# Two quotient buffers in a quantised feed-forward, its tile loop reordered, and its weights turned earlier

## The reference

```
x = x + attention_0(layernorm(x), ctx)      # 16 heads of 16, softmax, biases
x = x + experts(layernorm(x))               # 32 experts + 8 zero experts, 6 per token
x = x + attention_1(layernorm(x), ctx)
x = x + fp4_ffn(layernorm(x))

def fp4_quant_dequant(x):                   # blocks of 16 along the last dimension
    scale = maximum(max(abs(xb)) / 6, 1e-12)
    idx = searchsorted([.25,.75,1.25,1.75,2.5,3.5,5], abs(xb / scale))
    return [0,.5,1,1.5,2,3,4,6][idx] * sign(xb) * scale

gate, up = fp4_linear(x, w_gate), fp4_linear(x, w_up)     # 256 -> 704
fp4_linear(silu(gate) * up, w_down)                       # 704 -> 256
```

## Time and profile before

| what | value |
|---|---|
| median of 3 runs | 998.67 us (998.26 to 1001.34) |
| the profiled execution | 1005.61 us, its span 1003.8 us |
| mean granted TensorE clock | 0.951 |
| TensorE busy | 898.1 us, 89% |
| VectorE busy | 626.4 us, 62% |
| ScalarE busy | 437.4 us, 44% |
| GpSimd busy | 304.1 us, 30% |
| feed-forward, from the weights' turns to the last sum | 837.8 to 1001.4 us |

### The profile page before, as it was taken

The page is one execution under the profiler, slowest core; times in us unless marked ns, Lnnn a source line. Parts: engine busy times, 40 slices in busy tenths (PEclk is TensorE's granted clock), DMA queues, the critical chain, the costliest instruction groups (busy, mean ns, idle before and its releaser), DMA issues.

```text
span 1003.8 us, 19829 instructions
## 1 busy us (share of the span) xinstructions
PE 898.1 (89%) x7228; PEld 685.1 (68%) x7228; DVE 626.4 (62%) x1317; ACT 437.4 (44%) x946; POOL 304.1 (30%) x311
## 2 busy tenths in 40 slices
PE   2997799999997978999999967799999996699996
PEld 1764687878876747878888844587878874366664
DVE  3455577878854594545545465566777764678872
ACT  0442466666664561111111112466666675345442
POOL 8003466767782260000000004000000001476673
PEclk9998799999998798999999977999999999999998
DMA  9788644444333469121111204345565500000000
GB/s 258 219 238 203 113 93 92 93 93 93 62 106 98 138 214 250 46 67 32 32 32 48 65 3 82 74 85 112 107 117 109 106 27 21 0 11 16 16 10 22
DMA packets 98157, 90.45 MB, mean 90 GB/s; under 512 B 43554, under 2 KB 85410, under 8 KB 97954
## 3 DMA queue, kind: packets, MB, share of 16 engines
q1 hardware_dynamic: 98066, 89.25, 36.6%
HBM read 69.36 MB, written 19.63 MB: 89 GB/s over the span
## 4 chain that ended last, share of the span: by engine, by line
PE 72%; DVE 12%; DMA 5%; POOL 3%; ACT 3%; issue 2%; SPq 2%; DVEq 0%; POOLq 0%; ACTq 0%
PE ps L988 13%; PE ps L805 8%; PE ps L859 8%; PE ps L791 8%; PE ps L994 7%; PE ps L819 7%; PE ps L1062 3%; DMA Qz<-mT 3%; PE ps L709 3%; PE ps L1078 2%; PE ps L868 2%; POOL Pr L645 2%; PE ps L779 2%; PE ps L828 1%; DMA X<-x_in 1%
## 5 line engine op out<-in xcount | busy, mean ns | idle before, releaser
L1444 DVE TENSOR_REDUCE ext<-ps 112x2 f32<-112x750 f32 x256 | 232.6, 933 | 66.5 <-PE ps L791 63.4
L1175 ACT ACTIVATE Pr<-ps 125x448 f32<-125x448 f32 x384 | 199.2, 542 | 88.5 <-PE ps L805 75.0
L805 PE MATMUL ps<-Qz,Kp 98*125 98x224 f16 x768 | 130.7, 265 | 14.0 <-DMA Qz<-mT 11.7
L791 PE MATMUL ps<-Kp,Qz 96*112 96x375 f16 x512 | 122.6, 332 | 5.8 <-DMA Qz<-qscr 4.9
L805 PEld LDWEIGHTS ps<-Qz,Kp 98*125 98x125 f16 x768 | 94.8, 137 | 47.2 <-DMA Qz<-mT 15.9
L859 PE MATMUL ps<-wv,ctx 128*125 128x256 f32 x384 | 120.7, 400 | 1.9 <-DVE xT L1417 1.0
L599 POOL TENSOR_TENSOR X<-X,bo 112x256 f32 x32 | 22.5, 724 | 284.6 <-DVE Pr L1362 233.0
L1585 DVE TENSOR_TENSOR Pr<-Pr,ps 128x336 f32<-128x336 f32 (+2 forms) x86 | 32.7, 381 | 88.9 <-ACT Pr L1257 73.8
L819 PE MATMUL ps<-Pr,Vx 125*32 125x112 f32 x3072 | 86.9, 261 | 0.0
L819 PEld LDWEIGHTS ps<-Pr,Vx 125*32 125x32 f32 x3072 | 71.4, 110 | 14.9 <-ACT Pr L1175 10.3
L1589 DVE SCALAR_TENSOR_TENSOR X<-ps,W,X 112x256 f32<-112x256 f32 x167 | 70.7, 477 | 17.3 <-PE ps L994 17.3
(11 more groups left out here) (176 smaller groups left out, 1417.1 us busy)
## 6 DMA issues: line engine op xcount, KB each, us to landing
ctx<-ctxT SPq DMA_DIRECT2D x56, 375.0 KB, 3.7
Kp<-kscr SPq DMA_DIRECT2D x96, 187.5 KB, 4.8
kscr<-ksp SPq DMA_DIRECT2D x24, 375.0 KB, 4.2
Pr<-wexp SPq DMA_DIRECT2D x20, 384.0 KB, 4.2
Qz<-qscr SPq DMA_DIRECT2D x174, 28.0 KB, 4.1
expert<-wexp SPq DMA_DIRECT2D x12, 384.0 KB, 3.9
Pr<-ctxT SPq DMA_DIRECT2D x8, 375.0 KB, 4.5
kscr<-Pr SPq DMA_DIRECT2D x8, 375.0 KB, 3.9
```

What stands on the lines that cost most here:

```text
L791: last = mm(ps[0:S, 2 * (p % 2) + u, 0:M], Qz[0:96, q0 + u * S:q0 + (u + 1) * S], Kp[0:96, k0:k0 + M], start=True, stop=True)
L805: last = mm(ps[0:KC, 4 + k % 2, u * 2 * S:(u + 1) * 2 * S], Kp[0:98, k0:k0 + KC], Qz[0:98, q0:q0 + 2 * S], start=True, stop=True)
L1175: A(Pr[g % 2][0:KC, j, GI * t:GI * t + GI, :].rearrange("r h q -> r (h q)"), ps[0:KC, 4 + k % 2, 0:GI * S], ACT.Exp, scale=scale).then_inc ...
L1444: V.tensor_reduce(ext[0:S, 2 * p:2 * p + 2], ps[0:S, 2 * (p % 2):2 * (p % 2) + 2, 0:M], AX_X, red).then_inc(row_maximum_taken, 1)
```

## The change

- **Two quotient buffers.** qrh and qch become pairs; h_over(i) waits only for h_back(i-2). Where the buffers lie is changed for this: x's quotients, xq and the second pair move to xT2f, the weights fgT, fuT and fdT to expert and key buffers of the SBUF that are free by then.
- **The order.** GpSimd and VectorE get new passes; h_over(i+1) comes ahead of h_back(i), gate_h(i+1) ahead of h_round(i), h_exponents(i) first. h_over(0) comes ahead of pass 0. ScalarE's and TensorE's passes keep their order.
- **The weights' turns** move from the end of the second attention into its front: "weight" in PE_FRONT and ACT_FRONT, in PSUM banks 6 and 7; project_group(1) waits for the last of their copies. One of the turns is cut differently, twelve as before.
- **The first tile.** tile_norms(0, 10), x_scales(0), x_exponents(0), x_round(0) and x_scales(1) stand on VectorE ahead of the last normalise, x_magic(0) on ScalarE ahead of the last values_turned. The norms of tiles 10 to 13 come behind pass 0.

```diff
+FIRST = 10
-PE_FRONT = "turn project turn project turn R R project R R turn R R project R R M V V V V W W"
+PE_FRONT = "weight weight weight weight weight weight weight turn project weight weight weight weight weight turn project turn R R project R R turn R R project R R M V V V V W W"
+ACT_FRONT = "weight weight weight weight weight weight weight turned high weight weight weight weight weight turned high turned high turned high"
...
# GpSimd
-            def h_over(i):
+            def h_over(i, par):
                 pool.wait_ge(h_scales_ready, i + 1)
-                wait_from(pool, hq_ready, i)
-                over(qrh, hf, rch, NH, h_divided)
+                if not isinstance(i, int) or i >= 2:
+                    pool.wait_ge(hq_ready, i - 1)
+                over(qrh[par], hf, rch, NH, h_divided)
...
             def ffn_batch(i, par, left=3):
-                h_over(i)
                 if left >= 2:
                     x_back(i + 2, par)
                 if left >= 3:
                     x_over(i + 3)
+                if left >= 1:
+                    h_over(i + 1, 1 - par)
                 h_back(i, par)
...
             x_over(2)
+            h_over(0, 0)
             ffn_batch(0, 0)
...
# TensorE
+                def turn_weights(k):
+                    if k == 0:
+                        pe.wait_ge(weights_quantised, B)
+                    if k >= 2:
+                        pe.wait_ge(weights_copied, k - 1)
...
                     pe.wait_ge(group_xT_copied, q + 1)
+                    if q == 1:
+                        pe.wait_ge(weights_copied, len(TURNS))
...
-            pe.wait_ge(weights_quantised, B)
-            for k, (w, pieces) in enumerate(TURNS):
...
-            pe.wait_ge(weights_copied, len(TURNS))
...
# ScalarE, behind the last sums of each attention
+                if l == 1:
+                    x_magic(0)
                 values_turned(g0 + B - 1)
...
# VectorE
+                if l == 1:
+                    tile_norms(0, FIRST)
+                    x_scales(0, 0)
+                    x_exponents(0)
+                    x_round(0)
+                    x_scales(1, 1)
                 normalise(g0 + B - 1)
                 residual(g0 + B - 1, B - 1)
...
             def ffn_batch(i, par, left=3, sums=True):
+                h_exponents(i, par)
                 if left >= 2:
                     x_exponents(i + 2)
-                if sums:
-                    ffn_sum(i - 2)
-                h_exponents(i)
                 if left >= 3:
                     x_scales(i + 3, 1 - par)
+                if sums:
+                    ffn_sum(i - 2)
                 if left >= 2:
                     x_round(i + 2)
-                h_round(i)
                 if left >= 1:
                     gate_h(i + 1, 1 - par)
+                h_round(i, par)
```

More of the change, by code:

```diff
@@ L883, in _ @@
                     values = iter([(j, c) for j in range(NJ) for c in range(C2)])
-                    turns, projects = iter(range(NG)), iter(range(NG))
+                    turns, projects, weights = iter(range(NG)), iter(range(NG)), iter(range(len(TURNS)))
                     for step in ((PE_FRONT if l else PE_FIRST) if b < 0 else PE_ORDER).split():
-                        if step == "turn":
+                        if step == "weight":
+                            turn_weights(next(weights))
+                        elif step == "turn":
                             turn_group(next(turns))
@@ L1158, in _, with weights_out @@
                 else:
[L1159 to L1167, removed]
+                    def weights_out(k):
+                        w, pieces = TURNS[k]
+                        act.wait_ge(weights_turned, k + 1)
+                        a, c, _ = pieces[0]
+                        if w < 2:
+                            n = sum(FCH[a] for a, _, _ in pieces)
+                            A((fgT, fuT)[w][c][:, 128 * a:128 * a + n], ps[:, 6 + k % 2, 0:n], ACT.Copy).then_inc(weights_copied, 1)
+                        else:
+                            n, r = len(pieces) // 2, FCH[c]
+                            at = D * (c % 3)
+                            A(own_expert[c // 3][0:r, at:at + 256 * n], ps[0:r, 6 + k % 2, 0:256 * n],
+                              ACT.Copy).then_inc(weights_copied, 1)
@@ new lines, in _ @@
+                    weights, turned, high = iter(range(len(TURNS))), iter(range(NG)), iter(range(NG))
+                    for step in ACT_FRONT.split():
+                        if step == "weight":
+                            weights_out(next(weights))
+                        elif step == "turned":
+                            q = next(turned)
+                            t = 4 if q else 0
+                            act.wait_ge(group_turned, q + 1)
+                            A(xTs[q], ps[:, t:t + 2, 0:QG * S], ACT.Copy).then_inc(group_xT_copied, 1)
+                        elif step == "high":
+                            q = next(high)
+                            act.wait_ge(group_projected, q + 1)
+                            for m in range(C2):
+                                last = A(qsps[:, q, :, m, 0, :], ps[:, (6 if q else 2) + m, 0:QG * S].rearrange(
+                                    "p (b q) -> p b q", q=S), ACT.Identity, bias=bqk[1][:, m:m + 1])
+                            last.then_inc(group_high_ready, 1)
@@ L1290, in h_turned, with ffn_batch @@
                 A(hT[0:64, 5, :], ps[0:64, 6, 2 * R:3 * R], ACT.Copy).then_inc(hqT_copied, 1)
[L1292 to L1306, removed]
+            def ffn_batch(i, par, first=False, left=2):
                 if left >= 2:
                     x_magic(i + 2)
-                h_magic(i)
+                h_magic(i, par)
                 if left >= 1:
@@ new lines, in exponents, with add_magic, x_exponents, x_round @@
+            def exponents(r, c, done):
+                V.tensor_scalar(c.bitcast(U32), r.bitcast(U32), 0x7F800000, None, ALU.bitwise_and).then_inc(done, 1)
+            def add_magic(r, c, done):
+                V.scalar_tensor_tensor(r, r, PRED, c, ALU.mult, ALU.add).then_inc(done, 1)
+            def x_exponents(i):
+                dve.wait_ge(x_divided, i + 1)
+                exponents(qrx, qcx, x_exponents_ready)
+            def x_round(i):
+                dve.wait_ge(x_magic_ready, i + 1)
+                add_magic(qrx, qcx, x_rounded)
@@ new lines, in h_exponents, with h_round, gate_h @@
+            def h_exponents(i, par):
+                dve.wait_ge(h_divided, i + 1)
+                exponents(qrh[par], qch[par], h_exponents_ready)
+            def h_round(i, par):
+                dve.wait_ge(h_magic_ready, i + 1)
+                add_magic(qrh[par], qch[par], h_rounded)
+            def gate_h(i, par):
+                dve.wait_ge(ffn_silu_ready, i + 1)
+                dve.wait_ge(ffn_up_ready, i + 1)
+                V.tensor_tensor(hf.rearrange("p (a b) -> p a b", a=2),
+                                sg.rearrange("p (a b) -> p a b", a=2), ps[:, 2:4, 0:FI // 2],
+                                ALU.mult).then_inc(h_gated, 1)
+                dve.wait_ge(h_gated, i + 1)
+                scales(hf, amh, sch[par], rch, NH).then_inc(h_scales_ready, 1)
@@ new lines, in ffn_sum, with ffn_batch @@
+            def ffn_sum(i):
+                dve.wait_ge(ffn_down_ready, i + 1)
+                xb = XT[:, bass.ds(i * D, D)]
+                V.tensor_tensor(xb, xb, ps[:, 7, 0:D], ALU.add).then_inc(ffn_added, 1)
+            def ffn_batch(i, par, left=3, sums=True):
+                h_exponents(i, par)
+                if left >= 2:
+                    x_exponents(i + 2)
+                if left >= 3:
+                    x_scales(i + 3, 1 - par)
+                if sums:
+                    ffn_sum(i - 2)
+                if left >= 2:
+                    x_round(i + 2)
+                if left >= 1:
+                    gate_h(i + 1, 1 - par)
+                h_round(i, par)
@@ L1637, in _ @@
                     V.memset(junk[:, :], 0.0).then_inc(experts_done, 1)
[L1639 to L1663, removed]
-                                        rstd[:, bass.ds(i, 1)], ALU.subtract, ALU.mult))
-                scales(xn[0], amx, scx[par], rcx, NX).then_inc(x_scales_ready, 1)
@@ L1718, in _ @@
-            FIRST = T - 2
-            for t in range(FIRST):
-                if LAST_OF[t] > B - 5:
-                    tile_stats(t)
-            tile_norms(0, FIRST)
-            x_scales(0, 0)
-            x_exponents(0)
-            x_round(0)
-            x_scales(1, 1)
             x_exponents(1)
```

139 lines of the change are left out of this document (63 added, 76 removed).

## The result

The changed kernel took 1021.38 us (median of 4 runs, 1015.70 to 1023.04) beside 1000.00 us for the kernel before (4 runs, 998.26 to 1002.96): ratio 1.0201, 95% interval 1.0152 to 1.0249. It is slower, as forecast, by 1.5 to 2.5%; the forecast time was 1012.7, so that 21.4 us were lost where 14.0 had been forecast. The profiled execution took 1020.68 us, its span is 1018.9 us, 15.1 us more than before.

What follows compares the result with a forecast made beforehand. The prediction took a loop of GpSimd and VectorE, 9.36 us a tile, to bound the kernel. Terms 18.4 + 0 + 2.2 - 3.0 - 3.6 = +14.0 us on 998.67 gave 1012.7, range 1000 to 1023.

Steps and rivals of the forecast that it cites:

- the forecast's loop: Tile loop: up, gate_h, h_over, h_back, turn_h, then up again; 10.53 us, 11.2 with interference, +18.4 us in ten periods.
- h_over's 0.53 us of interference: Tile loop: h_over on GpSimd runs beside VectorE's h_round and comes 0.53 us later.
- the step "that decides": TensorE's unchanged pass queues up(i+1) behind turn_h(i-1), which waits for h_back(i-1), closing a loop over one tile.
- the rival that the text gave 20%: Tile loop: full exclusion or a longer chain through exponents and ScalarE; period 11.6 to 12, +18 to +21 us; 20%.
- The rival's own sum: Chain from h_over through ScalarE: 5.8 us, under the 6.5 of h_back, turn_h and up, unless x_exponents waits 1.5 more.
- The 0.15 us for h_exponents and h_back: Tile loop: h_exponents(i+1) and h_back(i)'s first half are released together; 0.15 us taken from the range 0 to 0.5.
- its pair: Profiled VectorE rounding (1.25 us) beside a GpSimd product (1.15 against 0.62 apart), read as a wait shorter than full exclusion.
- The fill: First tiles, up(1) to up(3): 24.8 us against 25.2 before, taken as 0, ends -1.5 and +2.
- The drain: End of the tile loop: h_back(12) comes behind h_over(13); +2.2 us, ends 0 and +3.
- part 3: Tile 0 begun inside the attention: normalise(15) late, but gate(0) at 846.5 instead of 850.07; -3.6 us, ends -1.5 and -4.3.
- the signs that the prediction names: Among them: TensorE idle about 2 us ahead of turn_h, period 11.0 to 11.4, first gate product about 846 less front's gain.
- Part 2: Weights turned in the second attention's front, keeping TensorE busy so two projections run at full clock; -3.0 us, ends -4.6 and +1.5.

Runs made afterwards that it cites:

- silu_first: Changed kernel with silu of gate(i+1) ahead of x_magic(i+2) and h_magic(i) on ScalarE: ratio 1.0121 to the kernel before, period 11.14 us.
- weights_only: Changed kernel with the old tile loop and tile 0 begun behind the attention again, weights' turns still in the front: 998.55 us, ratio 0.9948 to the kernel before.
- turn_late: Changed kernel with turn_h(i-1) behind up(i+1) on TensorE, gate_h's scales waiting for h_back(i-2): ratio 1.0184 to the kernel before, period 11.30 us.
- old_loop: Changed kernel with the earlier tile-loop order on GpSimd and VectorE, moved weights and early tile 0 kept: 993.79 us (0.9936), again 994.50 us (0.9924).

## Why the prediction was right, and where it was not

**The period.** 11.2 us was forecast and 11.31 measured; ten periods cost 19.4 us, not 18.4. The terms of the forecast's loop held nearly to the hundredth: h_over's 0.53 us of interference was 0.51. But the step "that decides" was named wrongly. The loop through turn_h is real, and 11.14 us long (silu_first); the one 0.2 us longer was the mechanism of the rival that the text gave 20%: h_over, then h_exponents and x_exponents each held for a GpSimd instruction, x_magic, h_magic, silu, gate_h. That the sum came out is in part luck: it is right by the second longest of two nearly level chains.

The rival's own sum went wrong in two places. It counts 2.29 us from h_over's end to 925.01, which is silu's start, and sets the 5.8 us that come of it beside the 6.5 until gate_h's product; silu's own 0.74 us is missing, and with it the two were level already. And x_exponents did wait for another GpSimd instruction, in every tile, which the text names but leaves out of the 5.8. Measured, from h_over's end at 909.96: h_exponents ended at 911.98, 1.45 us late, x_exponents at 913.37, 1.2 later than its own 0.29 us asks for, then x_magic, h_magic and silu to 916.79. Up had ended at 916.52. The rival's period, 11.6 to 12, was too long by at least 0.3 all the same, since x_magic's two passes held h_magic up for 0.95 us (913.41 to 914.36), not 1.76, and GpSimd held h_exponents for 1.45.

**The lock.** The Trainium skill, "SBUF — State Buffer", "Who interferes with whom", says that the later of two contending instructions waits for the whole of the other. The traces agree, in both directions. First h_exponents in the kernel before, with GpSimd idle; then the pair in the changed kernel:

```profile
922.75 0.53 DVE L1668 TENSOR_SCALAR Pr<-Pr 128x704 uint32<-128x704 uint32 x1 [1.08 <-POOL Pr L645]
```

```profile
943.91 1.67 POOL L671 TENSOR_TENSOR xT<-xT 128x704 f32<-128x704 f32 x1
943.98 1.98 DVE L1443 TENSOR_SCALAR Pr<-Pr 128x704 uint32<-128x704 uint32 x1 [1.27 <-POOL Pr L648]
```

The exponents started when 1.60 us of GpSimd's instruction were left, and took 1.45 more than alone. H_over started at 908.06, when 0.67 us of the rounding of 907.90 were left, and took 0.51 more. Both were held for what was left of the other, less 0.15 or 0.16 us. So the forecast's 0.53 was nearly right, but not because the wait is shorter than the rule has it, as the prediction reads its pair: that product started at 925.72, 0.58 us behind the rounding, and what was left was 0.67 us, not 0.9. The 0.15 us for h_exponents and h_back was a guess in the range 0 to 0.5 and came true in the loop through turn_h by another pair: the second half of h_back, 1.55 us instead of 1.39, started before h_exponents had ended.

**The fill** was given 0 and cost 1.7 us: gate_h(2) came 13.58 us behind gate_h(1) (11.83 before), since the norms stand ahead of the exponents of pass 1 and GpSimd's h_back lengthened two of them (1.13 and 1.23 us instead of 0.17). **The drain**, +2.1 for +2.2, held, and so did **part 3**, -3.4 for -3.6, in the stretch to gate(0). Of the signs that the prediction names, TensorE's idle time ahead of turn_h was 1.35 us, not 2; the first gate product came at 843.25.

**Part 2** was given -3.0 and brought -4.5 in this trace, but not in the way that was forecast. Of the two front projections at half clock, the first stayed slow (5.37 us) and the second took 4.85 instead of 6.22; then the values at 633 ran slow, and at 637 the front had saved only 0.3 us. The forecast of 3.3 us for each projection failed here. In other traces of kernels with the weights in the front it came true for one of the two. The first projection of weights_only and the second of turn_late (5.49 and 6.22 us in the kernel before):

```profile
596.14 3.27 PE L801 MATMUL ps<-Pr,wq 128*128 128x448 f32 x8 [1.01 <-ACT Pr L1205]
```

```profile
603.99 3.27 PE L803 MATMUL ps<-Pr,wq 128*128 128x448 f32 x8 [1.01 <-ACT Pr L1207]
```

From the experts' end to the last turn_sums, the four traces with such a projection of 3.27 us (weights_only, turn_late and both of old_loop) took 239.0 to 240.3 us, the six others with the weights in the front 242.9 to 245.1, and the four without them 246.7 to 247.8. So the gain is sure, and its size depends on whether one projection ran at full clock; what decides that no run shows.

The gain common to all ten came in the first sequence of the attention, where nothing was changed. Waits of TensorE there, in the kernel before and in weights_only:

```profile
649.50 0.60 PE L805 MATMUL ps<-Qz,Kp 98*125 98x224 f16 x4 [2.06 <-DMA Qz<-mT]
```

```profile
646.33 0.60 PE L827 MATMUL ps<-Qz,Kp 98*125 98x224 f16 x4 [0.22 <-DMA Qz<-mT]
```

and the windows behind them, of the kernel before (clock 0.66) and of weights_only (1.00):

```profile
650.00:655.00 5.00, 5.00 (x25) 4.03 (x24) 2.21 (x3) 3.04 (x6) 0.00 (x0) 0.66 0.82 137
```

```profile
645.00:650.00 5.00, 4.78 (x32) 3.81 (x32) 3.83 (x5) 3.28 (x7) 0.00 (x0) 1.00 0.76 163
650.00:655.00 5.00, 5.00 (x78) 4.15 (x75) 4.43 (x8) 3.88 (x10) 0.00 (x0) 1.00 0.49 68
```

The small transfer of the maxima landed late, TensorE idled 2 us, and its clock fell. In all ten traces of kernels with the weights in the front the wait was 0.2 us and the clock stayed at 1.00; in all four without, the wait was 1.9 to 2.3 us and the clock behind it fell to 0.66 to 0.72. Why this transfer of 3.5 KB lands sooner (1.7 us from its issue in the changed kernel, 2.6 in the kernel before, medians of two) is not shown by any run: that stays open, and with it why this part of the gain, for which nothing was forecast, came with the moved weights.

**The time.** 1021.4 against 1012.7: of the 8.7 us, 1.3 are the base (1000.0 instead of 998.67); the terms above were 1.1 us (the spans changed by 15.1, the sum said 14.0) off; the remaining 6.3 are that the execution profiled before was a high one and the one after a slightly low one. That the terms come so near is itself partly luck: part 2 brought 1.5 us more than forecast, the stretch from gate(0) to gate_h(0) another 1.4, and the loop, the fill and the start of the span cost 3.8 more.

## What to carry to other kernels

- When a step is moved ahead in one queue, follow every chain that passes through it once around, from a step's end to the same step's end, and write down all that come within 5% of the longest. Cutting one of two level chains gives nothing (0 and 0.2 us), cutting both gave 1.2 us a tile, and either alone would have looked like a refutation.
- The wait that a profile shows may be cured by one move of a short instruction (x_round, 0.36 us, ahead of 2 us of others: a period of 8.9 us instead of 9.3) where a second buffer and a new order cost 2 us a tile.
- Exponents and roundings on VectorE and products on GpSimd ran one behind the other when both were released at one moment: count the later one's wait in every chain that it lies on. Whether other work between them would hide the wait was not tested.

## What was not expected of the hardware

Behind a wait of 1.9 to 2.3 us of TensorE in the attention its granted clock fell in the next 5 us, four times in four, while the tile loop of the changed kernel, with a wait of 1.35 us in each period, kept 1.00 from 880 to 990. The length of the wait alone does not decide: in the fill of the kernel before, TensorE waited 2.15 us ahead of 866.12, its clock was 1.00 in every 2 us from 864 to 876, and the next gate took the 2.63 us that it takes in the loop at full clock.

```profile
866.12 0.44 PE L1056 MATMUL ps<-ident,Pr 128*128 128x128 f32 x2 [2.15 <-POOL Pr L645]
867.11 2.63 PE L1062 MATMUL ps<-Pr 128*128 128x352 f32 x8 [0.55 <-ACT Pr L1280]
```

And where GpSimd goes on to its next instruction at once and VectorE has to be released by the one just ended, GpSimd came first, in all nine tiles between 880 and 980 of the changed kernel: VectorE's 0.53 us exponents ended 1.98 us after their start, and the 0.29 us exponents behind them took 1.47.
